# ODE stage: 28 columns per matmul instead of 4, 24 of them zeros, and one scan per chunk

## The reference

```python
def _mlp(y, W1, b1, W2, b2, W3, b3):
    h = jnp.tanh(y @ W1.T + b1)
    h = jnp.tanh(h @ W2.T + b2)
    return h @ W3.T + b3
def _rk4_step(y, dt, params):
    f = lambda z: _mlp(z, *params)
    k1 = f(y)
    k2 = f(y + dt / 2 * k1)
    k3 = f(y + dt / 2 * k2)
    k4 = f(y + dt * k3)
    return y + dt * (k1 + 2 * k2 + 2 * k3 + k4) / 6
y0 = x[:, 0]
_, ys = jax.lax.scan(interval, y0, None, length=S - 1)
```

## Time and profile before

| | |
|---|---|
| median of 3 timed runs | 7892.87 us |
| the profiled execution, its own time | 7864.81 us |
| its span | 7863.0 us |
| PE, matmuls | busy 7113.7 us (90%), 201,621 |
| PEld, weight loads | busy 6454.8 us (82%), 201,621 |
| DVE | busy 3692.3 us (47%) |
| ACT | busy 3045.9 us (39%) |
| matmuls of the ODE loop (line 842) | 196,224, from 884.0 to 6630.6 us |

### The profile page before, as it was taken

One profiled execution on the slowest core, in us unless ns is written; L12 is line 12 of the kernel. 1 busy time (PEld: TensorE's weight loads), 2 busy tenths in 40 slices (PEclk: granted clock), 3 DMA queues, 4 the chain that ended last, 5 costly groups with the idle time before them and its releaser, 6 DMA issues. The chain is left out here.

```text
span 7863.0 us, 452418 instructions
## 1 busy us (share of the span) xinstructions
PE 7113.7 (90%) x201621; PEld 6454.8 (82%) x201621; DVE 3692.3 (47%) x16941; ACT 3045.9 (39%) x18260; POOL 1245.4 (16%) x5237
## 2 busy tenths in 40 slices
PE   8896699999999999999999999999999998547886
PEld 3231599999999999999999999999999997436775
DVE  5344444444444444344444444444444443539997
ACT  2232233333333333333333333333333332328886
POOL 1000122112212222122212221222112221010001
PEclk7685555555555555555555555555555555668887
DMA  1000000100010000100010001000100000012332
GB/s 48 0 1 20 32 5 5 43 5 5 5 43 5 5 5 11 37 5 5 5 43 5 5 5 43 5 5 5 43 5 5 5 23 6 0 48 112 117 118 82
DMA packets 45133, 189.84 MB, mean 24 GB/s; under 512 B 7155, under 2 KB 27318, under 8 KB 33030
## 3 DMA queue, kind: packets, MB, share of 16 engines
q1 hardware_dynamic: 38662, 145.18, 4.8%
q0 software_dynamic: 4480, 15.38, 0.6%
HBM read 122.93 MB, written 37.62 MB: 20 GB/s over the span
## 5 line engine op out<-in xcount | busy, mean ns | idle before, releaser
L842 PE MATMUL p<-H,W 128*128 128x4 f16 x130816 | 5324.2, 167 | 70.9 <-ACT h L925 30.3
L842 PEld LDWEIGHTS p<-H,W 128*128 128x128 f16 x130816 | 4918.9, 105 | 92.5 <-issue 35.5
L993 DVE TENSOR_TENSOR_SCAN L<-H,h 128x24 f16<-128x24 f16 x8176 | 1694.6, 208 | 3245.7 <-ACT h L925 1910.8
L842 PE MATMUL p<-L,W2D 128*128 128x4 f16 x32704 | 2122.0, 168 | 60.4 <-issue 55.3
L842 PE MATMUL p<-L,W13D 128*128 128x4 f16 x32704 | 2111.5, 168 | 15.8 <-issue 13.4
L842 PEld LDWEIGHTS p<-L,W2D 128*128 128x128 f16 x32704 | 1743.5, 104 | 81.1 <-issue 62.4
L842 PEld LDWEIGHTS p<-L,W13D 128*128 128x128 f16 x32704 | 1742.4, 104 | 28.3 <-issue 19.5
L925 ACT ACTIVATE H<-p 128x8 f16<-128x8 f32 x4088 | 758.0, 186 | 1854.6 <-PE p L842 1854.5
L932 ACT ACTIVATE H<-p 128x8 f16<-128x8 f32 x4088 | 759.4, 186 | 1810.9 <-PE p L842 1736.6
L925 ACT ACTIVATE h<-p 128x8 f32<-128x8 f32 x4088 | 724.3, 177 | 4.4
L932 ACT ACTIVATE h<-p 128x8 f32<-128x8 f32 x4088 | 719.3, 176 | 0.0
(11 more groups left out here) (378 smaller groups left out, 4817.2 us busy)
## 6 DMA issues: line engine op xcount, KB each, us to landing
e_W<-w_scaled SPq DMA_DIRECT2D x23, 2304.0 KB
e_W<-w_scaled SPq DMA_DIRECT2D x23, 1152.0 KB, 5.3
raw_f<-in_spline SPq DMA_DIRECT2D x21, 1024.0 KB, 6.8
w_scaled<-raw_f SPq DMA_DIRECT2D x7, 2304.0 KB, 8.9
w_scaled<-raw_f SPq DMA_DIRECT2D x7, 1152.0 KB, 11.1
raw<-in_spline POOLq DMA_DIRECT2D x3, 1024.0 KB, 7.0
rows_in<-zeros POOLq DMA_DIRECT2D x4, 768.0 KB, 11.8
e_xs<-rows_in SPq DMA_DIRECT2D x12, 256.0 KB, 5.7
```

Of the source, the lines that this page charges most:

```text
L842: ins = pe.matmul(out[:, m, 0:B], weights, x, start=False, stop=(left[m] == 0 and n == len(terms) - 1), skip_group_check=True)
L993: sg.up(dve.tensor_tensor_scan(flat(cols(L, GROUPS[n])), flat(cols(H, GROUPS[n])), flat(cols(h, GROUPS[n])), -1.0, ALU.mult, ALU.add), f"l ...
```

## The change

H1, H2, L1 and L2 become [128, 4 chunks, 28 columns, 3]: columns 0 to 3 hold the sequences as before, columns 4 to 27 are zeros that are written once. Each matmul of a product streams all 28 columns of a chunk and accumulates into 28 columns of PSUM, of which 24 stay zero. POOL sets the zeros before the loop, and the matmuls that clear p1 and p2 ahead of it clear 28 columns too. ACT writes the same 4 columns of each chunk, and H2 is treated like H1. Since the columns of two chunks no longer lie side by side, the scan of a group is cut into one scan of 12 elements per chunk; the second of the two signals.

```diff
+    WIDE = 28
...
-        H1, H2 = sb("H1", [P, NV, 3], F16), sb("H2", [P, NV, 3], F16)
+        H1, H2 = sb("H1", [P, KH, WIDE, 3], F16), sb("H2", [P, KH, WIDE, 3], F16)
...
-        L1, L2 = sb("L1", [P, NV, 3], F16), sb("L2", [P, NV, 3], F16)
+        L1, L2 = sb("L1", [P, KH, WIDE, 3], F16), sb("L2", [P, KH, WIDE, 3], F16)
...
+            for x in (H1, H2, L1, L2):
+                sg.up(pool.memset(x[:], 0.0), "zeros")
+            sg.wait(pool, "zeros", 5)
             for x in (H1, H2):
-                sg.up(pool.memset(x[:, :, 1], LIFT), "zeros")
-                sg.up(pool.memset(x[:, :, 2], 0.0), "zeros")
+                sg.up(pool.memset(x[:, :, 0:B, 1], LIFT), "zeros")
...
-                columns = slice(B * k, B * k + B)
-                terms = [(W[:, q, k, P * m:P * m + P], H[:, columns, 0]) for q in range(NP)] if part == "h" else [
-                    (WD[:, k, P * m:P * m + P], L[:, columns, 1])]
+                terms = [(W[:, q, k, P * m:P * m + P], H[:, k, :, 0]) for q in range(NP)] if part == "h" else [
+                    (WD[:, k, P * m:P * m + P], L[:, k, :, 1])]
                 for n, (weights, x) in enumerate(terms):
-                    ins = pe.matmul(out[:, m, 0:B], weights, x, start=False, stop=(left[m] == 0 and n == len(terms) - 1), skip_group_check=True)
+                    ins = pe.matmul(out[:, m, 0:WIDE], weights, x, start=False, stop=(left[m] == 0 and n == len(terms) - 1), skip_group_check=True)
...
-                                for x in (H1, h1):
-                                    sg.up(act.activation(mb(cols(x[:, :, 0], q)), sums(p1[:, q[0]:q[-1] + 1]), ACT.Tanh, scale=factor[c]), "h1")
+                                for x in (H1[:, q[0]:q[-1] + 1, 0:B, 0], mb(cols(h1[:, :, 0], q))):
+                                    sg.up(act.activation(x, sums(p1[:, q[0]:q[-1] + 1]), ACT.Tanh, scale=factor[c]), "h1")
...
             def low(H, h, L, layer, e, n, w):
                 wait(dve, f"h{layer}", 2 * (G * e + n + 1), w)
-                sg.up(dve.tensor_tensor_scan(flat(cols(L, GROUPS[n])), flat(cols(H, GROUPS[n])), flat(cols(h, GROUPS[n])), -1.0, ALU.mult, ALU.add), f"lo{layer}")
+                for k in GROUPS[n]:
+                    ins = dve.tensor_tensor_scan(flat(L[:, k, 0:B, :]), flat(H[:, k, 0:B, :]), flat(cols(h, (k,))), -1.0, ALU.mult, ALU.add)
+                sg.up(ins, f"lo{layer}")
```

More of the change, by code:

```diff
@@ L737, in flow @@
         wb3, hb = sb("wb3", [P, KH]), sb("hb", [P, NV])
-        r, y1, b2s, zero = sb("r", [P, 4, NV]), sb("y1", [P, NV]), sb("b2s", [P, NV]), sb("zero", [P, B], F16)
+        r, y1, b2s, zero = sb("r", [P, 4, NV]), sb("y1", [P, NV]), sb("b2s", [P, NV]), sb("zero", [P, WIDE], F16)
         third, minus, twice, base = sb("third", [P, NV]), sb("minus", [P, NV]), sb("twice", [P, NV]), sb("base", [P, NV])
@@ L868, in _ @@
             sg.wait(pe, "rest", 2)
-            sg.wait(pe, "zeros", 1)
+            sg.wait(pe, "zeros", 7)
             for x in (p1, p2):
                 for m in range(KH):
-                    ins = pe.matmul(x[:, m, 0:B], W2[:, 0, m, 0:P], zero[:], start=True, stop=True)
+                    ins = pe.matmul(x[:, m, 0:WIDE], W2[:, 0, m, 0:P], zero[:], start=True, stop=True)
                 sg.up(ins, "cleared")
@@ L913, in _ @@
                 sg.up(act.activation(wd[:], whole[:, 0], ACT.Copy, scale=1.0 / LIFT), "part")
-            sg.wait(act, "zeros", 5 + 2 + 8)
+            sg.wait(act, "zeros", 7 + 2 + 8)
             def steps(scale, factor):
@@ L930, in steps @@
                                 wait(act, "u2", G * e + n + 1, w)
-                                for x in (H2[:, :, 0], h2[:, e, :, 0]):
-                                    sg.up(act.activation(mb(cols(x, q)), sums(p2[:, q[0]:q[-1] + 1]), ACT.Tanh, scale=scale), "h2")
+                                for x in (H2[:, q[0]:q[-1] + 1, 0:B, 0], mb(cols(h2[:, e, :, 0], q))):
+                                    sg.up(act.activation(x, sums(p2[:, q[0]:q[-1] + 1]), ACT.Tanh, scale=scale), "h2")
             sg.wait(act, "large_set", 1)
@@ L988, in _ @@
             dve.tensor_copy(sums(p2), mb(b2s[:])).then_inc(sg.sem["ready"], 1)
-            sg.wait(dve, "zeros", 5 + 2 + 8)
+            sg.wait(dve, "zeros", 7 + 2 + 8)
             def low(H, h, L, layer, e, n, w):
                 wait(dve, f"h{layer}", 2 * (G * e + n + 1), w)
-                sg.up(dve.tensor_tensor_scan(flat(cols(L, GROUPS[n])), flat(cols(H, GROUPS[n])), flat(cols(h, GROUPS[n])), -1.0, ALU.mult, ALU.add), f"lo{layer}")
+                for k in GROUPS[n]:
+                    ins = dve.tensor_tensor_scan(flat(L[:, k, 0:B, :]), flat(H[:, k, 0:B, :]), flat(cols(h, (k,))), -1.0, ALU.mult, ALU.add)
+                sg.up(ins, f"lo{layer}")
             with dve.Fori(0, STEPS // UN) as i:
```

## The result

The changed kernel took 7926.17 us (median of 8 runs, 7910.32 to 7967.1) against 7896.17 us for the kernel before (8 runs, 7856.9 to 7902.01). The ratio is 1.0049, with a 95% interval of 1.0027 to 1.0071. So it is slower, where 7864 and a small gain were forecast. The profiled execution has a span of 7922.8 us, 59.8 more than before, and nearly all of that is in the ODE loop: from the first to the last of its 196,224 matmuls it takes 5809.8 us, before 5746.6, so 63.2 more. That is one execution of each: the one of the kernel before lies 31 us under the median of its eight runs, the one after 2 us under its own, so the medians are only 30 us apart. Differences of some 30 us (0.02 us for a packet of instructions) between profiled loops can be the spread of the runs.

What follows compares the result with a forecast made beforehand. PE's loads and the chain balance at 1.34 us per product, with instruction packets a third limit. After the change packets decide: 3.72 x 1533 = 5703 us, 44 less, 15 given back, so 7892.87 - 29, about 7864; range 7720 to 8130.

Steps and rivals of the forecast that it cites:

- The clock rises: TensorE in the ODE loop: with 28 columns streamed after each load, the clock goes from 0.50 to near 1.00.
- the falls back: ODE loop: stretches in which the clock drops again because PE idles 0.6 us in every 3.67; 15 us given back.
- A load follows the clock. So 27 ns would become 13.3: PE's weight loads in the loop: distance between matmul starts falls from 27 ns to 13.3 at full clock.
- the clock rises, the pace of the loads does not: Rival for PE in the loop: full clock but slow loads, chain 1.42 us at worst, total 7880 to 8050; chance 0.13.
- The chain's path: From one product's last sums to the next's: ACT, scans, L, 21 matmul distances, back to ACT; 1.13 us at full clock.
- The second scan, +0.07: DVE's extra scan per group: L ready after 0.28 instead of 0.21 us, adding 0.07 to the chain, up to 0.15.
- The sizes of the streaming and the rest: 24 more columns at half clock cost 20 ns per product; DVE has idle time enough for 8176 more scans.
- A packet takes PE about 3.67 us however fast PE is: TensorE's instruction queue: each packet of 128 matmuls takes about 3.67 us, so packets decide the loop's time.
- The rival in which packets come every 3 us with a faster PE: Instruction queue no limit: work decides at 3.01 + 0.05 us per packet, -1056 us, total 6837; chance 0.16.
- the 13 to 16 matmuls in 0.25 us: Narrow windows of the loop: read as the number of matmuls PE starts in 0.25 us outside the dips.
- The dips: Narrow windows of the loop: PE falls to 9, 1, 10 and 9 matmuls, 4.0, 3.75 and 3.75 us apart, awaiting instructions.
- The few waits of 1 to 4 us: Longest instruction waits in the loop: an estimated 75 of 117.5 us, about 0.05 us per packet.

Runs made afterwards that it cites:

- e6: Kernel before without the matmuls on the remainder part of W2 and W13, 32 per product instead of 48: 7143.96 us, beside 7915.9 for the kernel before.
- e2: Changed kernel with one scan per group again, zeros on both sides of each pair of chunks: 7917.6 us, ratio to the kernel before 0.9995.
- e3: Changed kernel with 4 columns per matmul instead of 28, keeping the second scan: 8006.6 us, ratio to the kernel before 1.0128.
- e4: Changed kernel with 16 columns per matmul instead of 28: 8040.49 us, ratio to the kernel before 1.0156.
- e1: Kernel before with six stretches of fp16 matmuls, 4 to 64 columns, added ahead of the loop: starts 25.0 ns apart at full clock up to 28 columns.
- e5: e2 without the matmuls on the remainder part of W2 and W13, 32 per product instead of 48: 7247.48 us, beside 7915.9 for the kernel before.

## Why it is slower: the forecast's steps, one by one

What decided is in one table, from the matmuls' starts in each profile. A step of the integration is 8 products, 384 matmuls, so exactly three packets, and the waits for instructions recur at the same three matmuls of every step, 128 apart (in e6 a step is two packets). An edge "with a wait" is one with over 0.1 us from the last start to the next. The work in a packet is the median step without such an edge, divided by three (in e6 by two). The mean packet leaves out those of over 5 us, which hold a wait of microseconds: 25 in each loop, 176 to 178 us in all, before and after alike (in e6 those of over 5.5 us, 18).

| | clock | product, us | work in a packet | mean packet | rest | edges with a wait |
|---|---|---|---|---|---|---|
| before, 4 columns, one scan | 0.50 | 1.334 | 3.591 | 3.694 | 0.103 | 42% |
| e2, 28 columns, one scan | 0.91 | 1.322 | 3.536 | 3.720 | 0.184 | 54% |
| e3, 4 columns, two scans | 0.50 | 1.393 | 3.747 | 3.776 | 0.029 | 9% |
| after, 28 columns, two scans | 0.96 | 1.376 | 3.704 | 3.735 | 0.031 | 8% |
| e4, 16 columns, two scans | 0.50 | 1.400 | 3.773 | 3.803 | 0.030 | 10% |
| e6, 32 matmuls per product | 0.50 | 1.206 | 4.864 | 4.881 | 0.017 | 2% |

The change added 0.113 us of work to a packet and the waiting gave 0.072 back. The remaining 0.041, for the 1508 ordinary packets, is 62 us of the 63.2 that the loop is longer. With two scans the work is a little more than 2 2/3 products, because the second and the sixth product of a step are regularly longer (1.43 and 1.42 us in the changed kernel).

- **The clock rises: right.** 1.00 for 5381 of the loop's 5810 us, 0.50 for the other 429. The 280 products in the middle of which the clock was 0.50 have a median of 1.420 us, the others 1.378; by that the falls back cost some 12 us, an estimate (15 in the forecast).
- **"A load follows the clock. So 27 ns would become 13.3": wrong, and this is the step that failed.** It was taken from two fp32 stretches, whose starts are 110 and 220 ns apart, far above the 25 ns of e1, and carried over to fp16. In its place e1 measured 25.0 ns at full clock. The forecast's own pieces with this one number put right, 0.25 + 0.03 + 0.28 + 0.06 + 21 x 0.025 (0.525) + 0.2 + 0.03, give 1.375 us; measured 1.376. With that the chain is no longer far under the packet, as the forecast had it, but about as long, and it decides. So the rival "the clock rises, the pace of the loads does not" came true, inside its 7880 to 8050. The sentence beside it, worked out from the Trainium skill's floor, had the chain at 1.38.
- **The chain's path: the wrong group, with the right sum by luck.** The forecast adds up group 1's path, 21 distances behind its L. But the wait that holds PE is that for group 0's L, as shown with the result. In the changed kernel that path is 0.057 to the first matmul on L, 0.497 for the 19 distances to group 0's last one, 0.182 for that one, 0.096 to the tanh, 0.250 for ACT, 0.032 to the scan and 0.264 for the two scans: 1.378 us (medians). The same sum gives 1.339 before, 1.324 in e2 and 1.393 in e3. So the pace won 0.032 here, the wider last matmul took 0.016 of it back, and the second scan cost 0.056.
- **The second scan, +0.07: right in size.** e3 has 0.059 in the chain, and e3, without the rise of the clock, is 1.3% slower than the kernel before.
- **The sizes of the streaming and the rest.** 24 columns at half clock cost 0.020 us (0.02 in the forecast). DVE had the idle time, as assumed: 2936 us busy in the loop.
- **A packet takes PE about 3.67 us however fast PE is: right in kind, the size stays open.** In e1 13 packets with 3.20 us of work each took 3.62 on average; e2's mean of 3.72 also holds packets that came in time. In the forecast's sum, with its 0.05, they give 3.67 x 1533 = 5626 us and 3.77 x 1533 = 5779, 121 less and 32 more than before. So whether a halved pace would have brought a gain stays open, since no kernel here had such a pace; e2, whose chain became a little shorter, stayed at 0.9995. The rival in which packets come every 3 us with a faster PE has nothing for it (e1's shortest is 3.45). The Trainium skill's "mostly hidden" (Runtime: NRT & Kernel Launch, Instruction fetch mechanics) does not hold in e1, where PE stands 0.36 us at a boundary with nothing else to wait for; in e6, with 4.86 us of work in a packet, it does. One reading in the forecast is wrong without harm: the 13 to 16 matmuls in 0.25 us are those under way in a window, while PE starts 8 to 10. The dips are real: there the starts are 137 to 483 ns apart, four times, 128 matmuls from one to the next.
- **The few waits of 1 to 4 us** were put at 75 us; 177 less 25 ordinary packets of 3.7 is 84.

That the packets, not the chain, hold e2 back rests on e1 (the limit without a chain), e2 (a shorter chain; 742 gaps of over 0.15 us between matmuls at the packets' edges, 486 before, and 76 elsewhere in both) and e6 (more work per packet, hardly any waits). In the changed kernel, with a wait at 8% of the edges, the chain decides. Why the queue delivers a packet in some 3.45 us at times and in 3.73 at others stays open.

## What to carry to other kernels

Before buying clock for TensorE, find out what sets the distance between its starts: in short matmuls with a load each it was 27 ns at 1.2 GHz and 25 at 2.4, so the clock was worth 0.04 us per product, less than the 0.06 us by which one more small scan lengthened the chain. Where a long straight program keeps PE busy with matmuls of that size, count instructions: 128 matmuls with their loads were one packet and took 3.62 us on average in e1, where PE needed 3.20 for them. Only fewer matmuls per product (e5, e6) moved the time much, at the price of the low half of the weights; in e6 some 530 of the loop's 715 us came from the shorter chain and the rest from the waits that vanished. Add up a chain along the wait that really ends last, which here was group 0's. A duration read from another data type bounds a step; it does not size it.

## What the runs showed that was not expected

- fp16 matmuls with a load each start 25.0 ns apart at full clock with 4 as with 28 columns, gapped or packed, and 29 ns with 64.
- At half clock 28 columns hide beside the load almost wholly: 26.9 ns in e1, and 0.020 us for a whole product in e5 against e6.
- The granted clock stayed at 0.50 with 16 columns in 48 matmuls per product (e4) and with 28 in 32 (e5), and was 1.00 for most of the loop with 28 in 48 (after).
- The waits for instructions came in steps: in e1's long stretch distances at a packet's edge were 265, 540, once 140 at the start and once 813 ns, beside 25 elsewhere.
